# Moving ScalarE's splitting copies of the rotary queries and keys one to five heads later

## The chip, the cores and the metric

One core of a Trainium2 chip runs the whole kernel as one program. The metric is the device time of one execution in microseconds: the kernel before took 1350.16 us (median of 3 runs, 1348.41 to 1352.78). The engines are TensorE (PE), VectorE (DVE), ScalarE (ACT), GpSimd (POOL) and SyncE (SP), which issues most transfers. Each has its own instruction queue, runs it strictly in order, and waits on semaphores that the other engines and the transfers raise.

## The reference

Two layers of a gated decoder on x (8 sequences of 256 rows, 256 features). Layer 0 is a decoder block (masked self-attention, cross-attention, feed-forward) and a mixture of experts, top 2 of 8. Layer 1, cut to what matters here:

```
x = x + tanh(g_xattn[1]) * rotary_cross_attention(layernorm(x), ctx, key_mask)
x = x + tanh(g_ffn[1])   * moe_top1_of_8(layernorm(x))

q = larope(x @ Wq + bq);  k, v = split(ctx @ Wkv + bkv);  k = larope(k)
attn = softmax(q k^T / 8, masked keys off);  out = (attn v) @ Wo + bo      # 16 heads of 16 features
```

`larope` turns each pair of features by an angle that grows with the position: te*cos - to*sin, te*sin + to*cos.

## The kernel before

The stage of the change is the function `rotary_and_experts`: the rotary cross-attention of layer 1, sequence by sequence, and then the top-1 experts on sorted rows. The order of all engines in it is written out by hand as loops over a **beat** b (0 to 7, the sequence whose softmax is made) and within it a **head** h (0 to 15). In head h of beat b TensorE makes the transposed scores of (b, h) (`scores_T`, L1228) and the plain scores of a head eight further on (`scores`, L1210: sequence b+1, head h+8, or from h = 8 on sequence b+2, head h-8). VectorE takes their row maxima (L1774), and ScalarE makes the exponential of the transposed scores (`exps`, L1491). TensorE may start `scores_T` of head h once the exponential of head h-2 is done (two banks). Between the heads stand the other steps of several sequences:

- sequence b+3, queries: TensorE's product at h = 0 (L1177), VectorE's rotation at h = 0 (L1758, L1760), then the **split** in three bf16 parts, so that scores in bf16 keep float32 precision: GpSimd adds the two halves (`whole`, L1603), ScalarE copies to bf16 (`first_part`, L1467), GpSimd makes the remainder (`rest`, L1608), ScalarE copies it (`second_part`, L1472), GpSimd makes the third part (`third_part`, L1613).
- sequence b+3, keys: product and rotation at h = 4, the same split.
- sequence b+3, values: product at h = 8 (`project_values`, L1200), ScalarE's copy (`value_rows`, L1484), GpSimd's column of ones (`keep_values`, L1631).
- sequence b-1: heads are transposed at h = 6, ScalarE copies them (`bring_heads`, tile `aT`, L1460), output product at h = 12. Several products share two banks in a fixed rotation; the value product of h = 8 needs the bank that `bring_heads` empties.
- sequence b+4: rows are transposed at h = 10; ScalarE copies them (`bring_rows`, L1454).
- sequence b-2: new row norm, whose inverse roots GpSimd makes in fourteen small operations (`inverse_roots`, L134 to L141, from beat 2 on), and VectorE applies at h = 9. Routing of sequence b-3 follows, with GpSimd's scatter (L1639).
- at h = 1, 5, 9, 13 ScalarE copies out four heads' attention output (`outputs`, L1497), which TensorE transposes two heads later (L1259).

GpSimd's order in a beat is: roots of sequence b+4, the whole split of the queries (sum, remainder, third part), roots of sequence b-2, the whole split of the keys, `keep_values`, from beat 4 on weight loads of the experts (`load_expert`, L1049 and L1050, 2 MB per expert; expert 0 in beat 4, experts 1 to 3 in beat 5), then the scatter.

SP's order in beat b is: query stacks, key stacks and key row of sequence b+2 (`stack`, L1066 and L1069, loads from DRAM in the layout that the scores want; they wait for the end of beat b-1 and for the parts' writes to have landed), the write of the query parts of b+3 to DRAM (`spread_parts`, L1077, waits for the third part), the two small transfers of the maxima (L1081, L1082), the write of the key parts of b+3, in beat 0 two further small ones (L1132, L1133), and from beat 2 on the rows of sequence b-2 kept for the router (L1087, two transfers). The first use of the stacks of sequence b+2 is `scores` at h = 8 of beat b.

ScalarE in head h does its exponential, then the split steps, then `bring_heads`, `bring_rows`, router copies and `outputs`.

Of the kernel before, what the change touches and what calls it, by code (L numbers as in the profile page):

```python
# [970 lines left out]
def rotary_and_experts(nc, tag, c, mem, X, Y, L, gate, x_dram, gate_f, ids_dram, rows_dram, out, w1_in, w2_in, b1_in, b2_in, wg_in, bg_in):  # L971
# [10 lines left out]
    with ExitStack() as ctx:  # L982
# [466 lines left out]
        def _(act):  # L1449
            def bring_rows(m):  # L1450
                if m >= 1:
                    act.wait_ge(*full("q", m - 1))
                act.wait_ge(*full("x", m))
                nc.scalar.activation(flat(xT[:, :, :]), bank_of("x", m)[:, :], ACT.Copy).then_inc(emptied("x", m), 1)  # L1454

            def bring_heads(m):
                if m >= 1:
                    act.wait_ge(*full("z", m - 1))
                act.wait_ge(*full("a", m))
                nc.scalar.activation(flat(aT[:, :, :]), bank_of("a", m)[:, :], ACT.Copy).then_inc(emptied("a", m), 1)  # L1460

            def first_part(m, side):
                f, parts, at = ((fq, pq, q_place), (fk, pk, k_place))[side]
                act.wait_ge(f_sum[side], m + 1)
                if m >= 1:
                    act.wait_ge(spread[side], 16 * m)
                nc.scalar.activation(flat(parts[:, at[0], :, :]), f[:, :], ACT.Copy).then_inc(part1[side], 1)  # L1467

            def second_part(m, side):
                r, parts, at = ((rq, pq, q_place), (rk, pk, k_place))[side]  # L1470
                act.wait_ge(rest1[side], m + 1)
                nc.scalar.activation(flat(parts[:, at[1], :, :]), r[:, :], ACT.Copy).then_inc(part2[side], 1)  # L1472

            def value_rows(m):
                p = m % 4
                act.wait_ge(*full("v", m))
                if m >= 4:
                    act.wait_ge(pv_done, QUADS * (m - 3) + 2)
                if m == 0:
                    act.wait_ge(ready0, 1)  # L1480
                    act.wait_ge(kept_in, 1)
                for u in range(NU):
                    rows = V[:, p, u, 0:H * VW].rearrange("p (h e) -> p h e", e=VW)
                    ins = nc.scalar.activation(rows[:, :, 0:DK], bank_of("v", m)[:, u * D:(u + 1) * D].rearrange("p (h e) -> p h e", e=DK),  # L1484
                                               ACT.Copy, scale=mcf[:, m * NU + u:m * NU + u + 1])
                ins.then_inc(emptied("v", m), 1)

            def exps(m, h):
                act.wait_ge(st_ready, H * m + h + 1)
                act.wait_ge(pv_done, QUADS * m + h // 4 + 1)  # L1490
                nc.scalar.activation(PT[h % 8], bankT[h % 2][:, :], ACT.Exp).then_inc(exp_done, 1)  # L1491

            def outputs(g):
                act.wait_ge(pv_done, g + 3)
                if g >= 2:
                    act.wait_ge(*full("o", g - 2))
                nc.scalar.activation(OTS[:, g % 2, :], bankO[g % 2][:, 0:SEQ], ACT.Copy).then_inc(ot_out, 1)  # L1497

            def bring_router(n):
                act.wait_ge(*full("t", n))  # L1500
                if n >= 1:
                    act.wait_ge(*full("l", n - 1))
                nc.scalar.activation(flat(yT[:, :, :]), bank_of("t", n)[:, :], ACT.Copy).then_inc(emptied("t", n), 1)

            def probabilities(n):
                act.wait_ge(centred, n + 1)
                nc.scalar.activation(expd[:, :, :], expd[:, :, :], ACT.Exp).then_inc(prob_done, 1)
# [43 lines left out]
            for b in range(0, M):  # L1551
                for h in range(H):
                    exps(b, h)
                    if has(b + 3):
                        if h == 2:
                            first_part(b + 3, 0)
                        if h == 4:
                            second_part(b + 3, 0)
                        if h == 6:
                            first_part(b + 3, 1)  # L1560
                        if h == 8:
                            second_part(b + 3, 1)
                            value_rows(b + 3)
                    if h == 6 and has(b - 1):
                        bring_heads(b - 1)
                    if h == 10 and has(b + 4):
                        bring_rows(b + 4)
                    quad = QUADS * b + (h - 5) // 4
                    if h == 6 and early(b - 3):
                        probabilities(b - 3)  # L1570
                    if h == 15 and early(b - 2):
                        bring_router(b - 2)
                    if b == M - 1 and h == 12:
                        bring_router(EARLY_ONES - 1)
                    if h in PV_AT and 0 <= quad < QUADS * M:
                        outputs(quad)
# [1208 lines left out]
```

## Time and profile before

| what | value |
|---|---|
| median of 3 runs | 1350.16 us (1348.41 to 1352.78) |
| profiled execution | 1353.81 us, its span 1352.0 us |
| TensorE busy | 1181.2 us, 87% |
| VectorE busy | 786.6 us, 58% |
| ScalarE busy | 624.9 us, 46% |
| GpSimd busy | 554.8 us, 41% |
| mean granted TensorE clock | 0.945 |

Times in the rows are microseconds from the start of the span. Beat 0 begins at 948.9 (ScalarE's first exponential), beat 2 at 993.5, beat 5 at 1076.6, and the last beat ends near 1142. The span is the time from the first to the last instruction; the execution is 1.8 us longer. An entry in brackets is the engine's idle time just before the instruction and what ended it. `L_W` is the big memory that holds stacks, parts and, later, expert weights, so many tiles print by this one name; the line number tells them apart.

### The profile page before, as it was taken

The page shows a single profiled execution, that of the slowest core. Times are in us where ns is not written, and L with a number is a line of the kernel's source. Part 1 is how long each engine was busy: PE and PEld are TensorE (multiplying, and loading weights), DVE is VectorE, ACT ScalarE, POOL GpSimd, SP SyncE. Part 2 cuts the span into 40 slices and gives each one's busy share as a digit, 9 for nine tenths or more (in the row PEclk, how much of TensorE's full clock was granted, in tenths as well). Part 3 has the DMA queues.
Part 4 walks back from the last instruction along what each step waited for, and adds up shares of the span by engine and source line. Part 5 has one row for each costly group of instructions (what it writes and reads, how often), then busy time and mean ns, then how long its engine had stood idle before and what let it go on. Part 6 is the DMA issues. An engine that isn't in the chain of part 4 may idle for free. (4 is left out here: it accounts for less than half of the span.)

```text
span 1352.0 us, 27251 instructions
## 1 busy us (share of the span) xinstructions
PE 1181.2 (87%) x8333; PEld 944.7 (70%) x8333; DVE 786.6 (58%) x2994; ACT 624.9 (46%) x1515; POOL 554.8 (41%) x927
## 2 busy tenths in 40 slices
PE   4599999999997999899999999346988868689996
PEld 3366667676654888789999999333656645689995
DVE  4588878888873488855333333226868866532231
ACT  2268777888885332233333333011555535233331
POOL 3334454545433344545333333145454433433431
PEclk9799999999997999999999999776899989899998
DMA  4766674545411971132222222287434785511110
GB/s 107 176 128 169 144 171 101 116 98 117 97 36 22 378 197 33 48 45 36 37 41 35 37 40 31 40 180 176 100 84 114 152 248 188 188 34 48 39 36 6
DMA packets 116790, 137.64 MB, mean 102 GB/s; under 512 B 25739, under 2 KB 103065, under 8 KB 111740
## 3 DMA queue, kind: packets, MB, share of 16 engines
q1 hardware_dynamic: 101416, 106.73, 33.3%
q0 software_dynamic: 15232, 29.17, 9.6%
q8 instruction: 70, 1.15, 0.4%
q14 instruction: 72, 0.59, 0.2%
HBM read 102.51 MB, written 35.97 MB: 102 GB/s over the span
## 5 line engine op out<-in xcount | busy, mean ns | idle before, releaser
L765 DVE CUSTOM_DVE_ANT_0 att_masked_scores<-att_S,Bm 128x256 bf16<-128x256 f32 x512 | 190.2, 419 | 38.2 <-PE att_S L507 26.7
L640 ACT ACTIVATE att_PT<-att_T 128x512 f32<-128x512 f32 x256 | 146.3, 591 | 50.1 <-PE att_T L529 46.2
L2401 ACT ACTIVATE moe_hT<-moe_H,moe_b 128x128 f32<-128x128 f32 x312 | 89.2, 369 | 170.2 <-PE moe_H L2314 168.9
L2326 PE MATMUL moe_Z<-moe_W,moe_hT 128*128 x624 | 141.6, 380 | 0.8 <-DVE moe_z L2626 0.8
L2489 POOL DMA_INDIRECT x<-Y,X x39 | 62.5, 1602 | 156.3 <-DVE Y L2637 152.0
L2326 PEld LDWEIGHTS moe_Z<-moe_W,moe_hT 128*128 128x128 f32 x624 | 115.5, 190 | 15.5 <-issue 1.2
L507 PE MATMUL att_S<-L_KS,L_QS 96*128 96x256 bf16 x512 | 99.2, 276 | 21.3 <-DMA L_KS<-att_k_dram 14.7
L1774 DVE TENSOR_REDUCE out_mx<-out_S 128x2 f32<-128x512 f32 x128 | 85.2, 685 | 28.6 <-PE out_S L1210 27.9
L529 PE MATMUL att_T<-L_QS,L_KS 99*128 99x256 bf16 x512 | 97.9, 273 | 4.0 <-ACT att_T L645 3.7
L2314 PEld LDWEIGHTS moe_H<-moe_aT,ff_w 128*128 128x128 f32 x832 | 96.8, 192 | 4.0 <-issue 2.1
L2314 PE MATMUL moe_H<-moe_aT,ff_w 128*128 128x128 f32 x832 | 97.2, 275 | 2.3 <-DVE X L2621 1.7
L2626 DVE TENSOR_TENSOR moe_z<-moe_Z,moe_b 128x256 f32<-128x256 f32 x39 | 16.6, 424 | 141.8 <-PE moe_Z L2326 141.8
L1525 ACT ACTIVATE X<-out_T,L_b 128x128 f32<-128x128 f32 x184 | 52.5, 369 | 97.6 <-PE out_T L1339 97.1
L1491 ACT ACTIVATE L_W<-out_T 128x512 f32<-128x512 f32 x128 | 72.6, 596 | 38.6 <-PE out_T L1228 38.0
L1339 PEld LDWEIGHTS out_T<-out_xT,L_w1s 128*128 128x128 f32 x736 | 86.6, 194 | 4.4 <-issue 1.9
L1339 PE MATMUL out_T<-out_xT,L_w1s 128*128 128x128 f32 x736 | 87.4, 278 | 2.7 <-DVE L_w1s L1915 1.4
L1352 PE MATMUL out_S<-L_W,X 128*128 x368 | 83.5, 380 | 2.4 <-DVE out_ys L1924 2.4
L645 ACT ACTIVATE att_T<-BmT 128x512 f32<-128x512 bf16 x127 | 76.4, 602 | 4.0
L1352 PEld LDWEIGHTS out_S<-L_W,X 128*128 128x128 f32 x368 | 68.1, 190 | 11.8 <-issue 3.5
L1210 PE MATMUL out_S<-L_W 97*128 97x256 bf16 x256 | 53.6, 297 | 24.4 <-DVE out_mx L1774 13.9
L507 PEld LDWEIGHTS att_S<-L_KS,L_QS 96*128 96x128 bf16 x512 | 45.9, 98 | 39.3 <-DMA L_KS<-att_k_dram 15.9
L529 PEld LDWEIGHTS att_T<-L_QS,L_KS 99*128 99x128 bf16 x512 | 49.4, 99 | 32.1 <-ACT att_T L645 6.8
(451 smaller groups left out, 2550.3 us busy)
## 6 DMA issues: line engine op xcount, KB each, us to landing
moe_W<-in_L_ffn_W SPq DMA_DIRECT2D x16, 1024.0 KB, 13.0
L_W<-in_L_ffn_W POOLq DMA_DIRECT2D x12, 1024.0 KB, 11.5
att_q_dram<-att_pq SPq DMA_DIRECT2D x16, 384.0 KB, 4.0
att_k_dram<-att_pk SPq DMA_DIRECT2D x16, 384.0 KB, 2.8
L_QS<-att_q_dram SPq DMA_DIRECT2D x16, 384.0 KB, 4.7
L_KS<-att_k_dram SPq DMA_DIRECT2D x16, 384.0 KB, 8.1
L_QS<-att_q_dram SPq DMA_DIRECT2D x16, 256.0 KB, 5.6
L_KS<-att_k_dram SPq DMA_DIRECT2D x16, 256.0 KB, 8.6
```

What stands on the lines that cost most here:

```text
L507: ins = nc.tensor.matmul(bankS[h % 2][:, u * SEQ:(u + 1) * SEQ], QS[0:ROWS, m % 3, h, u * P:(u + 1) * P], KS[0:ROWS, m % 3, h, :], start=T ...
L529: ins = nc.tensor.matmul(dst[:, u * SEQ:(u + 1) * SEQ], KS[0:ROWS_ALL, m % 3, h, u * P:(u + 1) * P], QS[0:ROWS_ALL, m % 3, h, :], start=Fa ...
L640: nc.scalar.activation(PT[:, h % 8, :], bankT[h % 2][:, :], ACT.Exp).then_inc(exp_done, 1)
L645: nc.scalar.activation(bankT[1][:, :], masks[layer][1][:, :], ACT.Copy).then_inc(seeded, 1)
L765: ins = nc.vector.tensor_tensor_reduce(masked_scores[:, h % 2, u, :], bankS[h % 2][:, u * SEQ:(u + 1) * SEQ], masks[m // B][0][:, u * SEQ: ...
L1339: ins = nc.tensor.matmul(bankH[half][:, f * P:(f + 1) * P], matrix[:, cc, k * P:(k + 1) * P], xT[:, s % 2, cc * P:(cc + 1) * P], start=(cc ...
L1352: ins = nc.tensor.matmul(bankY[:, 0:D], eT[:, s % 2, f * P:(f + 1) * P], matrix[:, f, :], start=(f == 0), stop=(f == NF - 1))
L1491: nc.scalar.activation(PT[h % 8], bankT[h % 2][:, :], ACT.Exp).then_inc(exp_done, 1)
L1774: nc.vector.tensor_reduce(mx[:, m % 2, :, h:h + 1], bankS[h % 2][:, :].rearrange("p (u k) -> p u k", u=NU), AXX, ALU.max).then_inc(max_don ...
L2314: ins = nc.tensor.matmul(bankH[half][:, f * P:(f + 1) * P], matrix[:, cc, g * P:(g + 1) * P], xT[:, s % 2, cc * P:(cc + 1) * P], start=(cc ...
L2326: ins = nc.tensor.matmul(bankZ[:, 0:D], eT[:, s % 2, f * P:(f + 1) * P], w2e[:, f, :], start=(f == 0), stop=(f == NF - 1))
L2401: ins = nc.scalar.activation(eT[:, s % 2, g * P:(g + 1) * P], bankH[half][:, f * P:(f + 1) * P], ACT.Relu, bias=b1[:, bass.ds(e * NF + g, 1)])
```

## The change

In beats 0 to 4 (those with a sequence b+3) ScalarE's four copies of the split move: queries' first part from head 2 to 3, queries' second from 4 to 6, keys' first from 6 to 9, keys' second from 8 to 13. `value_rows` stays at head 8. Nothing else is touched: the orders of TensorE, VectorE, GpSimd and SP are as before.

```diff
                 for h in range(H):
                     exps(b, h)
                     if has(b + 3):
-                        if h == 2:
+                        if h == 3:
                             first_part(b + 3, 0)
-                        if h == 4:
+                        if h == 6:
                             second_part(b + 3, 0)
-                        if h == 6:
+                        if h == 8:
+                            value_rows(b + 3)
+                        if h == 9:
                             first_part(b + 3, 1)
-                        if h == 8:
+                        if h == 13:
                             second_part(b + 3, 1)
-                            value_rows(b + 3)
                     if h == 6 and has(b - 1):
                         bring_heads(b - 1)
```

## Rows read from the trace of the kernel before

**Rows 1.** Windows: us, busy us (instructions) per engine, granted clock, DMA share, GB/s
```profile
993.50:1023.30 29.80, 24.49 (x184) 16.97 (x182) 20.33 (x54) 14.53 (x30) 12.85 (x36) 0.89 0.45 100
1076.60:1107.20 30.60, 19.04 (x169) 12.64 (x167) 18.30 (x56) 11.47 (x25) 9.71 (x22) 0.83 1.03 276
1009.40:1015.60 6.20, 6.20 (x30) 4.15 (x30) 1.52 (x4) 2.72 (x6) 2.08 (x4) 0.52 0.00 0
```

**Rows 2.** Timeline of ScalarE in beat 2, from head 6 on
```profile
1003.44 0.60 ACT L1491 ACTIVATE L_W<-out_T 128x512 f32<-128x512 f32 x1
1008.18 0.63 ACT L1467 ACTIVATE L_W<-L_W 128x512 bf16<-128x512 f32 x1 [4.15 <-POOL L_W L1603]
1008.72 0.58 ACT L1460 ACTIVATE out_aT<-out_A 128x512 f32<-128x512 f32 x1
```

**Rows 3.** Timeline of GpSimd in beat 2: third part, first root operation, sum
```profile
1001.85 1.17 POOL L1613 TENSOR_TENSOR L_W<-L_W 128x512 bf16<-128x512 f32 x1 [0.74 <-ACT L_W L1472]
...
1003.11 0.21 POOL L134 TENSOR_SCALAR out_ve<-out_mv 128x2 f32<-128x2 f32 x1
...
1006.89 1.26 POOL L1603 TENSOR_TENSOR L_W<-L_W 128x512 f32<-128x512 f32 x1
```

**Rows 4.** Timeline of TensorE in beat 2: value projection, head 12
```profile
1009.35 3.78 PE L1200 MATMUL out_A<-L_W 128*128 128x256 f32 x8 [4.13 <-ACT out_aT L1460]
...
1017.26 0.38 PE L1228 MATMUL out_T<-L_W 99*128 99x256 bf16 x2
```

**Rows 5.** Timeline of SP's transfer issues, beats 0, 1, 4 and 5
```profile
967.42 0.54 SPq L1132 DMA_DIRECT2D ids<-out_none  x1
...
970.17 1.25 SPq L1066 DMA_DIRECT2D L_W<-out_q_dram  x3
...
972.85 0.49 SPq L1069 DMA_DIRECT2D L_W<-key_off  x1
...
1052.42 0.52 SPq L1069 DMA_DIRECT2D L_W<-key_off  x1
...
1070.45 0.53 SPq L1077 DMA_DIRECT2D out_k_dram<-L_W  x1
...
1075.62 1.37 SPq L1066 DMA_DIRECT2D L_W<-out_q_dram  x3
```

**Rows 6.** Transfers, last column us to landing: key row in 969:974, in 1049:1054
```profile
L_W<-key_off SPq DMA_DIRECT2D x1, 8.0 KB, 9.1
...
L_W<-key_off SPq DMA_DIRECT2D x1, 8.0 KB, 12.0
```

**Rows 7.** Timeline of TensorE at head 8 of beats 1, 4 and 5
```profile
982.00 0.38 PE L1210 MATMUL out_S<-L_W 97*128 97x256 bf16 x2
983.12 1.99 PE L1200 MATMUL out_B<-L_W 128*128 128x256 f32 x8 [0.73 <-ACT out_aT L1460]
...
1064.92 0.38 PE L1210 MATMUL out_S<-L_W 97*128 97x256 bf16 x2
...
1096.00 0.58 PE L1210 MATMUL out_S<-L_W 97*128 97x256 bf16 x2 [9.85 <-issue]
```

**Rows 8.** All 16 parts' writes to DRAM (L1077)
```profile
DMA to landing us min/median/max: 2.7/3.0/13.9
```

**Rows 9.** Timeline of GpSimd: first half of load 0
```profile
1068.82 0.82 POOL L1049 DMA_DIRECT2D L_W<-in_L_ffn_W  x1
```

**Rows 10.** Timeline of ScalarE in beat 3: exponential of head 6
```profile
1036.28 0.60 ACT L1491 ACTIVATE L_W<-out_T 128x512 f32<-128x512 f32 x1
```

**Rows 11.** Timeline of TensorE in beat 3: head 12
```profile
1044.18 0.38 PE L1228 MATMUL out_T<-L_W 99*128 99x256 bf16 x2
```

**Rows 12.** Timeline of ScalarE: heads 11 to 13 of beat 0, head 13 of beat 4
```profile
967.12 1.67 ACT L1491 ACTIVATE L_W<-out_T 128x512 f32<-128x512 f32 x3
...
1073.20 0.60 ACT L1491 ACTIVATE L_W<-out_T 128x512 f32<-128x512 f32 x1 [1.80 <-PE out_T L1228]
```

**Rows 13.** SP's queue in 1084:1097: packets, MB, share of 16 engines
```profile
q1 hardware_dynamic: 282, 1.22, 40.8%
```

## The prediction

> **What bounds the kernel now.** I read the busy time by windows first, one window per rotary beat. Beats 2 and 5 stand out: 29.80 and 30.60 us long, TensorE busy 24.49 and 19.04 of them, at a mean granted clock of 0.89 and 0.83 [rows 1]. The question is what TensorE waits for there.
>
> Beat 2 is read from the timelines of three engines. ScalarE's exponential of head 6 starts at 1003.44. Next on its queue is the first part of the keys, which starts only at 1008.18, idle 4.15 us before it, released by GpSimd; behind that sits the copy `aT` (`bring_heads`), at 1008.72 [rows 2]. GpSimd explains the wait: the third part of the queries at 1001.85, then the fourteen small operations of the inverse root from 1003.11, then the sum of the keys at 1006.89, 1.26 us [rows 3]. TensorE's value projection needs the bank that `aT` empties: it starts at 1009.35, idle 4.13 before it [rows 4]. From 1009.4 to 1015.6 the granted clock was 0.52, the lower level of 1.2 GHz, behind those four idle microseconds [rows 1]; the projection took 3.78 us at that level [rows 4], and half of it, 1.9, would do at 2.4 GHz (the 1.99 of beat 1's row, [rows 7]). So the stall costs its own length and some 2 us more.
>
> Then the transfers. At the top of beat b SP reloads the stacks of sequence b+2: queries, keys, and last the key row (L1069). In beat 1 that row is issued at 972.85 and lands 9.1 us later, at 981.95 [rows 5, 6]; TensorE's first scores from it (head 8) start at 982.00 [rows 7]. In beat 4 it lands 12.0 us after its issue at 1052.42, so at 1064.4, and the scores start at 1064.92 [rows 5 to 7]. These loads arrive just in time: there is a hidden second bound. In beat 5 it shows: scores start at 1096.00, idle 9.85 [rows 7]. The key stack may go only when the key parts' write to DRAM (issued 1070.45, [rows 5]) has landed, and this one took 13.9 us, where the median is 3.0 [rows 8]: until 1084.35. Load 0 of the experts (2 MB by its shapes), which GpSimd issued at 1068.82 [rows 9], came ahead of it.
>
> **The change part by part.** No instruction is added or removed; ScalarE's order moves in beats 0 to 4.
>
> First part of queries, head 2 to 3: one exponential of 0.6 us goes before it, and its wait for GpSimd's sum shrinks by as much. TensorE runs ahead of ScalarE by two heads here and did not wait. I take 0; bounds 0 and -0.6 a beat, one exponential.
>
> First part of keys out of head 6. The second part of queries takes its slot, but needs only a remainder finished long before, so `aT` starts 0.63 us after the head-6 exponential and no longer after GpSimd. Beat 2: exponential ends 1004.04, second part to 1004.67, `aT` to 1005.25, projection at 1005.3 rather than 1009.35. But the GpSimd chain now starts later: third part of queries 1004.7 to 1005.9 (1.17, [rows 3]), roots 3.8 us (1003.11 to 1006.89) to 1009.8, sum 1.26 to 1011.1, first part of keys at head 9 to 1011.7, output copy 0.3, exponential of head 10 to 1012.6. TensorE's own work from the projection to head 12 took 7.9 us, 1009.35 to 1017.26 [rows 4], 6.2 of them at half clock; at full clock it is 4.8, so TensorE would be ready at 1010.1 and waits for that exponential: head 12 starts at 1012.65 instead of 1017.26 [rows 4], -4.6 us. Upper bound of the gain: head 12 right behind its own work, 1010.1, -7.2; lower: if the clock still falls, -3. I take -4.6, for every term of it is a row.
>
> Beats 3 and 4: the same chain, but the old stall was small there: from the exponential of head 6 to TensorE's head 12 it is 1036.28 to 1044.18, 7.9 us, in beat 3 [rows 10, 11], where beat 2 took 13.8. New in beat 3: second part of queries to 1037.5, third to 1038.75, roots to 1042.6, sum to 1043.9, first part of keys to 1044.6, copy 0.3, exponential of head 10 to 1045.5; head 12 starts 1045.6 instead of 1044.18. +1.4; bounds 0 (TensorE's lead of two heads hides it) and +2.8 (beat 4 pays it too; in my sum it is covered there by the late stacks). In beats 0 and 1 GpSimd has no such roots and the chain is 3.8 us shorter: 0. `bring_heads` is also earlier in beat 1, which the next term swallows.
>
> Second part of keys, head 8 to 13. This is the step with the price. Behind it on GpSimd stand the third part of the keys (1.2 us), the value columns, the scatters and load 0; behind that third part on SP stands the write of the key parts (L1077), and behind that write, in order, the rows kept for the router, both query stacks and the key stacks of the next beat. Before, SP issued that write long before the stacks (1070.45 and 1075.62 in beats 4 and 5, [rows 5]). Now:
>
> Beat 0 to 1: heads 11 to 13 end at 968.8 [rows 12]; second part to 969.4, third to 970.6, write issued 970.7 (0.53), two more transfers of 0.54 to 0.7 [rows 5], query stacks at 972.6 instead of 970.17 [rows 5], +2.4. Key row lands at 984.4 instead of 981.95, and TensorE had no slack: scores at 984.5 instead of 982.00. The projection behind them starts at 984.75 and not 983.12 [rows 7], so the net is +1.6; bounds 0 (the transfers overlap better) and +2.5.
> Beat 1 to 2: the same working, less the two extra transfers, gives query stacks 1.1 us later. Beat 2's head 8 may be that much later at no cost, since TensorE waits for ScalarE from 1010.1 to 1012.6 there. 0; bounds 0 and +1.
> Beats 2 to 5: head 13's exponential starts 2.4 us before the query stacks (1073.20 and 1075.62, [rows 5, 12]; the order of heads 13 to 15 is the same in beats 2 and 3); 0.6 + 0.6 + 1.2 us for the three steps and 0.5 + 1.2 for the write and the kept rows, with 0.1 at each handover, make 4.4: the stacks leave 2.0 later.
> Beat 3 has room for it: its head 6 comes 13 us after the top of the beat (1023.3 and 1036.28, [rows 10]), head 8 some 2.4 later, and from the first stack's issue to the last landing beat 1 took 11.8. 0; bounds 0 and +1.
> Beat 4 has none: landing 1066.4 instead of 1064.4, wanted at 1064.92, so +1.5; the scatter, which stands behind the third part on GpSimd, now falls into this load, for which I add 0.3. +1.8; bounds 0 and +4.
> Beat 5: from head 13 at 1073.20 second part to 1074.4, third to 1075.6, write issued 1075.65 and load 0 at 1076.05, 7.2 us later than its 1068.82. The write now starts ahead of the load, a plus. But load 0 no longer moves in the 7 us before the stacks; write, kept rows, query and key stacks, 0.4 + 0.5 + 0.8 + 0.8 = 2.5 MB by their shapes on SP's queue, now stand in front of beat 5's need together with load 0 and then loads 1 to 3. From 1084 to 1097 SP's queue moved 1.22 MB in 13 us beside the loads [rows 13], 94 KB/us. Some 0.3 MB (my estimate: one microsecond or two at the beginning) go before load 0 begins; 2.15 MB at 94 to 110 KB/us take 19.5 to 23 us from 1077.7: 1097 to 1101. If the small pieces are held back behind load 0 as before and the stacks begin at 1086, 1.54 MB end at 1100 to 1102. I take 1101, +5.0. Bounds: -5 (the early write lands in 3 us, key stacks leave at 1079 and land in 12, as in beat 4) and +11 (the rates fall to 70 KB/us, since beside load 0 the small pieces got less than the stacks do).
>
> Load order is where a rule bears. The row shows a write of 384 KB at 13.9 us beside load 0 against 3.0 at the median [rows 8]. The Trainium skill, "DMA: Bandwidth & Descriptors", section "Queues, rings and completion order", says that each engine alternates between queues a packet at a time, and that a semaphore's increment lands only after every earlier write of that engine, from whatever queue. By the second half, a write issued just ahead of load 0 would land unhindered, which makes the -5 end a rival; by the first, the stacks share with the loads from then on, which is the +5 term. The row of 13.9 us agrees with the rule; no row shows a write issued just ahead of a load.
>
> Sum: -4.6 + 1.4 + 1.6 + 1.8 + 5.0 = +5.2 us. Against the profiled execution's 1353.8: 1359.0. That execution lies 3.6 over the median of the runs, 1350.2; on the median: 1355.4.
>
> **The rivals.** No change: the write ahead of load 0 gives back what the later stacks lose, beat 5 starts its scores at 1096 as before, and the rest is +0.2: 1350.4. For it: every late term is of the size of beat 2's gain. Against: SP's queue holds 2.5 MB where it had 1.5.
> Faster: the write lands in 3 us as it does at its median [rows 8], key stacks leave at 1079 and land at 1091, and beat 4's load is not delayed beyond its slack: -4.6 + 1.4 + 1.6 + 0 - 5 = -6.6: 1343.6. It decides if load 0 yields to stacks that are already queued. For it: 13.9 us is four times the usual. Against: beat 4's loads took 12 us with no expert load beside them.
> Much slower: the stacks get only the smaller share until loads 1 to 3 are through, scores in beat 5 at 1107: +11 instead of +5: 1361.4. For it: the 1.22 MB in 13 us. Against: the stacks are then the larger of the two demands.
>
> **How the numbers follow.** Forecast 0.42, no change 0.21, faster 0.26, much slower 0.11. About 4 us, 0.3%, is what a measurement can tell from no change. The forecast lies just beyond it, so 0.05 of its 0.42 fall to "same"; of the 0.21 of no change, 0.02 fall to faster and 0.01 to slower. Faster 0.28, same 0.23, slower 0.49. The range, 1344 to 1361, runs from the faster rival to the much slower one; the forecast's own is 1351 to 1360.
>
> **What would show it.** Right: in beat 2 the idle time before the projection (L1200) is gone and the clock stays at 1.0; a wait of 2 to 3 us before the first keys part at head 9 in beats 2 to 4, on GpSimd's sum; SP's key write issued 1 to 2 us after ScalarE's second part; scores of head 8 idle 2 us in beat 1, on the key stacks. Wrong: beat 5's idle time under 8 us means that the order of write and load decides; beat 1 without that wait means that the stacks' landing does not follow their issue.

## The result, and the profile after

The changed kernel takes 1355.55 us (median of 22 runs), the kernel before, run beside it, 1350.15 (22 runs): ratio 1.0037, interval 1.0025 to 1.0049, so 5 us slower. The profiled executions are 1355.05 and 1353.81 us, only 1.2 apart, because the one of before was slower than any of its 22 runs (1344.19 to 1353.76). A second trace of each kernel was therefore taken, and the stage is read from all four.

First, by windows, beats 1 to 5 of the kernel after (us, busy us with instructions of TensorE, weight loads, VectorE, ScalarE, GpSimd, then granted clock, DMA share, GB/s):

```profile
970.50:993.30 22.80, 20.91 (x181) 15.00 (x179) 20.06 (x49) 13.85 (x28) 10.10 (x22) 1.00 0.50 114
993.30:1020.20 26.90, 23.76 (x184) 16.17 (x182) 21.63 (x55) 14.24 (x30) 12.86 (x36) 0.94 0.43 91
1020.20:1047.00 26.80, 23.62 (x195) 16.50 (x195) 24.52 (x69) 14.44 (x32) 13.58 (x37) 1.00 0.48 110
1047.00:1073.80 26.80, 22.80 (x193) 16.13 (x193) 22.34 (x64) 13.92 (x31) 12.32 (x26) 1.00 0.60 109
1073.80:1108.20 34.40, 19.13 (x169) 12.79 (x167) 18.41 (x56) 11.40 (x25) 12.65 (x25) 0.75 1.03 296
```

Against [rows 1], beat 2 went from 29.80 to 26.90 us and beat 5 from 30.60 to 34.40. In beat 5 TensorE does the same work and the rest is waiting.

**Beat 2** is read from three timelines, in the order of [rows 2 to 4]. ScalarE: `aT` (L1460) follows the exponential of head 6 at once, and the wait on GpSimd's sum stands before the first keys part at head 9 instead, 2.01 us:

```profile
1003.28 0.60 ACT L1491 ACTIVATE L_W<-out_T 128x512 f32<-128x512 f32 x1
1003.77 0.62 ACT L1472 ACTIVATE L_W<-L_W 128x512 bf16<-128x512 f32 x1
1004.29 0.59 ACT L1460 ACTIVATE out_aT<-out_A 128x512 f32<-128x512 f32 x1
...
1010.80 0.63 ACT L1467 ACTIVATE L_W<-L_W 128x512 bf16<-128x512 f32 x1 [2.01 <-POOL L_W L1604]
1011.34 0.37 ACT L1497 ACTIVATE out_OTS<-out_O 128x256 f32<-128x256 f32 x1
```

GpSimd: the third part now waits 3.52 us for ScalarE, and the root operations and the sum behind it are 2.6 us later than in [rows 3] (1004.47 for 1001.85, 1009.51 for 1006.89):

```profile
1004.47 1.15 POOL L1614 TENSOR_TENSOR L_W<-L_W 128x512 bf16<-128x512 f32 x1 [3.52 <-ACT L_W L1472]
...
1009.51 1.26 POOL L1604 TENSOR_TENSOR L_W<-L_W 128x512 f32<-128x512 f32 x1
```

TensorE: the projection (L1200) starts at 1005.54 with no wait for `aT`, 1.89 us long; head 12 starts at 1012.25. The wait has changed place: 1.39 us before L1259, whose input is the output copy queued behind the keys part:

```profile
1005.54 1.89 PE L1200 MATMUL out_A<-L_W 128*128 128x256 f32 x8
...
1011.76 0.44 PE L1259 MATMUL out_B<-ident,out_OTS 128*128 128x128 f32 x2 [1.39 <-ACT out_OTS L1497]
1012.25 0.39 PE L1228 MATMUL out_T<-L_W 99*128 99x256 bf16 x2
```

**Beat 5** starts at 1073.8 here and at 1076.6 in the trace before, so the issues are compared by their distance from it. SP issues the key write 1.1 us ahead of the beat (1072.73) instead of 6.2 (1070.45), and the query stacks 0.8 us into it (1074.63) instead of 1.0 ahead (1075.62) [rows 5], 1.8 later:

```profile
1072.73 0.38 SPq L1077 DMA_DIRECT2D out_k_dram<-L_W  x1
...
1074.63 2.03 SPq L1066 DMA_DIRECT2D L_W<-out_q_dram  x3
1076.76 2.18 SPq L1066 DMA_DIRECT2D L_W<-out_k_dram  x3
```

GpSimd issues the first half of load 0 at 1072.92, right after the write and not 1.6 us before it as in [rows 9]; against its beat that is 6.9 us later:

```profile
1071.56 1.15 POOL L1614 TENSOR_TENSOR L_W<-L_W 128x512 bf16<-128x512 f32 x1 [3.38 <-ACT L_W L1472]
...
1072.92 0.82 POOL L1049 DMA_DIRECT2D L_W<-in_L_ffn_W  x1
```

The transfers issued in 1072:1097 (last column: median us to landing) and, above them, what the two queues moved (packets, MB, share): the write lands in 2.8 us, where it took 13.9 [rows 8], but the stacks and the key row need 12.0 to 17.8 (before, 7.6 to 11.5):

```profile
q0 software_dynamic: 954, 3.46, 49.0%
q1 hardware_dynamic: 1648, 2.50, 46.0%
...
out_k_dram<-L_W SPq DMA_DIRECT2D x1, 384.0 KB, 2.8
L_W<-out_q_dram SPq DMA_DIRECT2D x1, 384.0 KB, 12.0
L_W<-out_k_dram SPq DMA_DIRECT2D x1, 384.0 KB, 15.9
...
L_W<-key_off SPq DMA_DIRECT2D x1, 8.0 KB, 17.8
```

TensorE at head 8 of beats 1, 4 and 5, to set beside [rows 7]: the wait of 9.85 in beat 5 is now 13.55, and beats 1 and 4 have short waits that were not there:

```profile
982.84 0.38 PE L1210 MATMUL out_S<-L_W 97*128 97x256 bf16 x2 [1.12 <-DMA L_W<-key_off]
983.06 1.89 PE L1200 MATMUL out_B<-L_W 128*128 128x256 f32 x8
...
1062.95 0.38 PE L1210 MATMUL out_S<-L_W 97*128 97x256 bf16 x2 [2.04 <-issue]
...
1096.87 0.59 PE L1210 MATMUL out_S<-L_W 97*128 97x256 bf16 x2 [13.55 <-issue]
```

### The profile page after: what moved, and what is told of

Its sections match the earlier page's. It is cut to its first block and busy times, and to the rows that moved or that the text cites. A ratio compares the mean times of both kernels' runs of the same rounds, so it can differ in the third digit from the quotient of the medians.

```text
span 1353.3 us, 27205 instructions
## 1 busy us (share of the span) xinstructions
PE 1174.0 (87%) x8287; PEld 942.8 (70%) x8333; DVE 789.0 (58%) x2994; ACT 623.8 (46%) x1515; POOL 554.4 (41%) x927
## 3 DMA queue, kind: packets, MB, share of 16 engines
q8 instruction: 70, 1.15, 0.4%
## 5 line engine op out<-in xcount | busy, mean ns | idle before, releaser
L529 PE MATMUL att_T<-L_QS,L_KS 99*128 99x256 bf16 x512 | 97.9, 273 | 11.5 <-ACT att_T L645 3.9
L1210 PE MATMUL out_S<-L_W 97*128 97x256 bf16 x256 | 54.0, 299 | 30.5 <-issue 15.6
```

The source lines that it names most:

```text
L529: ins = nc.tensor.matmul(dst[:, u * SEQ:(u + 1) * SEQ], KS[0:ROWS_ALL, m % 3, h, u * P:(u + 1) * P], QS[0:ROWS_ALL, m % 3, h, :], start=Fa ...
```

## All kernels by beat

Each beat is measured in the trace from ScalarE's first exponential to the next beat's first. "Stage" runs from beat 0's start to the last exponential; from there to the end of the span it is 210.2 to 211.4 us in every kernel. Heads are those of q1, q2, k1, k2 (first and second part of queries, then of keys). The ratio is to the kernel before, run in the same session.

| kernel | heads | beats 0 to 6 | stage | median us (runs) | ratio, interval |
|---|---|---|---|---|---|
| before | 2,4,6,8 | 21.9 22.7 29.8 27.2 26.2 30.5 18.2 | 192.6 | 1350.15 (22) | |
| same_before | 2,4,6,8 | 21.2 22.7 28.6 27.2 26.3 27.0 19.5 | 188.6 | 1352.89 (1) | |
| after | 3,6,9,13 | 21.8 22.9 26.8 26.8 26.8 34.4 18.2 | 193.9 | 1355.55 (22) | 1.0037, 1.0025–1.0049 |
| same_after | 3,6,9,13 | 22.1 25.2 25.2 26.8 29.9 33.3 19.3 | 198.0 | 1355.21 (11) | 1.0046, 1.0026–1.0065 |
| k2_at_10 | 3,6,9,10 | 22.6 22.7 28.0 27.9 26.3 31.1 18.2 | 192.8 | 1353.71 (12) | 1.0033, 1.0016–1.0050 |
| only_k2_at_13 | 2,4,6,13 | 21.9 25.0 28.5 26.9 27.3 34.3 18.2 | 198.3 | 1357.01 (7) | 1.0069, 1.0043–1.0094 |
| k_at_9_and_10 | 2,4,9,10 | 22.6 22.8 23.5 27.6 25.8 32.0 18.2 | 188.6 | 1345.74 (12) | 0.9975, 0.9959–0.9991 |
| k_at_9_and_13 | 2,4,9,13 | 21.5 23.0 22.9 26.6 26.6 34.0 18.2 | 189.0 | 1349.63 (12) | 1.0013, 0.9999–1.0028 |
| only_queries | 3,6,6,8 | 23.5 26.1 32.0 34.1 33.6 25.1 18.2 | 208.7 | 1368.59 (5) | 1.0146, 1.0125–1.0167 |
| load0_early | 3,6,9,13 | 22.1 25.7 25.2 26.8 27.5 27.7 18.2 | 189.2 | 1348.13 (12) | 1.0009, 0.9993–1.0024 |
| loads_wait | 3,6,9,13 | 21.4 23.1 26.6 26.9 29.2 27.5 19.0 | 189.4 | 1345.21 (12) | 0.9985, 0.9963–1.0006 |
| before_loads_wait | 2,4,6,8 | 21.9 22.7 29.4 27.2 26.1 22.7 19.1 | 184.8 | 1344.61 (12) | 0.9967, 0.9948–0.9986 |
| k_9_10_loads_wait | 2,4,9,10 | 22.6 22.6 23.5 27.6 25.8 22.6 19.4 | 180.8 | 1340.07 (9) | 0.9946, 0.9928–0.9965 |
| k_9_11_loads_wait | 2,4,9,11 | 20.7 22.2 22.5 27.3 26.6 23.2 19.5 | 177.9 | 1337.84 (6) | 0.9923, 0.9904–0.9941 |

The kernel before took 1349.1 us (29 runs) beside same_after, k2_at_10, only_k2_at_13 and k_at_9_and_10, 1347.5 (32) beside load0_early, loads_wait, before_loads_wait and k_9_10_loads_wait, and 1348.92 (17) beside the other four. Even the start of beat 0, ahead of which nothing differs, lies anywhere from 944.1 to 951.6: so one span says little, and beat lengths say more.

## The experiments

**The two kernels again.** No edit, same_after and same_before.

> The changed kernel again, unaltered, for a second trace and time. Theory (the late second part of the keys costs more in beat 5 than the freed head 6 gives back in beat 2): 1.002 to 1.005 times the kernel before; beat 2 shorter by about 3 us than the 29.8 before, idle time before beat 5's first scores (L1210) 13 to 15 us against 9.85. Rival (the +5 of the median is spread over the whole kernel and the beats are even, as the one profiled pair with its +1.3 suggests): beat 5 changes from trace to trace by as much as it differs from before.

> The kernel before again, unaltered, for a second trace of it. Theory (the profiled execution of before, 1353.8, was a slow one): the same waits at the same places, idle 4.1 us before beat 2's value projection and 9 to 10 us before beat 5's first scores, and a beat or two without a half-clock stretch that the first trace has or the other way round. Rival (beat 5's idle time is itself what varies): it is 7 us or less here.

Beat 5 waits 11.82 us in the second trace of after and 6.80 in that of before, in place of 13.55 and 9.85. So 13 to 15 us were not reached, and for before the rival came true: the wait of beat 5 itself varies by 3 us with the same code. TensorE, same_after:

```profile
1060.88 0.59 PE L1210 MATMUL out_S<-L_W 97*128 97x256 bf16 x2 [2.49 <-issue]
...
1096.84 0.37 PE L1210 MATMUL out_S<-L_W 97*128 97x256 bf16 x1 [11.82 <-issue]
```

and same_before:

```profile
1093.91 0.37 PE L1210 MATMUL out_S<-L_W 97*128 97x256 bf16 x1 [6.80 <-issue]
```

The shorter wait of same_before is not a faster write. The trace has no landing for it, but SP waited 6.0 us for it and could issue the key stacks only 12.6 us behind it (issued 1071.31):

```profile
1083.89 2.12 SPq L1066 DMA_DIRECT2D L_W<-out_k_dram  x3
```

What differs is the order behind it. Here the key stacks left 0.7 us ahead of GpSimd's load 1 (1084.58) and took 5.7 to 7.6 us; in the first trace they left at 1084.41, 0.7 behind it (1083.75), and took 7.6 to 10.1. That this order makes the 3 us is likely and not tested alone.

In beats 1, 2 and 4 what differs within one kernel is the clock. Windows of same_after:

```profile
967.20:992.50 25.30, 22.72 (x182) 16.02 (x182) 20.33 (x49) 14.13 (x30) 10.22 (x23) 0.93 0.47 102
992.50:1017.70 25.20, 21.99 (x184) 15.09 (x182) 21.58 (x54) 14.22 (x30) 12.90 (x36) 1.00 0.47 98
1044.40:1074.40 30.00, 25.47 (x193) 17.80 (x193) 22.43 (x64) 14.13 (x31) 12.75 (x26) 0.89 0.55 98
```

Here beats 1 and 4 ran partly at the lower level of 1.2 GHz, behind waits of 1.81 and 2.49 us, and beat 2 wholly at 2.4, behind a wait of 1.33 before L1259; in the trace of after it was the other way round (0.94 in beat 2, 1.00 in 1 and 4, behind 1.39, and 1.12 and 2.04). Such a beat is 1.6 to 3.1 us longer than in the other trace (26.8 for 25.2, 25.2 for 22.9, 29.9 for 26.8); in beats 1 and 4 the longer wait itself, 0.7 and 0.45 us, is in the difference. In beat 2 nearly all of it is one product: the eight matmuls of L1280 took 3.42 us in after and 1.97 in same_after. The mean stage of the two traces is 190.6 before and 196.0 after: +5.4, the same as the medians' +5.4. The traced pair alone gives +1.3.

**The second keys part alone, and its late place taken back.**

```diff
# k2_at_10: from after
-if h == 13:
+if h == 10:
     second_part(b + 3, 1)

# only_k2_at_13: from before (value_rows stays at h == 8)
-if h == 8:
+if h == 13:
     second_part(b + 3, 1)
```

> As the changed kernel, but the second part of the keys at head 10 instead of 13. Theory: the gain of beat 2 (-3) stays, and the write of the key parts, load 0 and the stacks go out about as before: beat 5's idle time back to about 10 us, so 3 to 4 us faster than the kernel before, 0.997. Rival 1 (ScalarE's and GpSimd's new chain at head 9 is what costs): no better than the changed kernel, 1.003. Rival 2 (any shift of load 0 costs): between them, 1.000.

> The kernel before with the second part of the keys alone moved, head 8 to 13. Theory: the loss without the gain: beat 5's idle time 13 to 15 us, beats 1 and 4 one to two us longer, beat 2 at its old 29.8; +6 to +9 us, 1.005 to 1.007. Rival (the late part is harmless, the loss sits in the new chain at head 9): 1.000.

Alone, the late part costs 1.0069, 9.3 us by the ratio and 7.9 between the medians, and shows all of the late terms: waits of 1.60 and 1.25 us in beats 1 and 4 and 11.83 us in beat 5, beside the old stall in beat 2 (3.33). TensorE, only_k2_at_13:

```profile
1012.59 0.80 PE L1200 MATMUL out_A<-L_W 128*128 128x256 f32 x1 [3.33 <-ACT out_aT L1460]
...
1068.64 0.38 PE L1210 MATMUL out_S<-L_W 97*128 97x256 bf16 x2 [1.25 <-issue]
...
1101.86 0.37 PE L1210 MATMUL out_S<-L_W 97*128 97x256 bf16 x1 [11.83 <-issue]
```

But k2_at_10 failed its expectation (0.997; measured 1.0033): taking the lateness back gains only 1.5 us on after. ScalarE of k2_at_10 shows the wait of head 9, and TensorE the two waits behind it, the second for the rows' copy:

```profile
1013.61 0.63 ACT L1467 ACTIVATE L_W<-L_W 128x512 bf16<-128x512 f32 x1 [2.52 <-POOL L_W L1604]
...
1014.57 0.44 PE L1259 MATMUL out_B<-ident,out_OTS 128*128 128x128 f32 x2 [1.89 <-ACT out_OTS L1497]
...
1016.77 0.45 PE L1280 MATMUL out_A<-L_wo,out_aT 128*128 128x256 f32 x1 [1.10 <-ACT out_xT L1454]
```

So something else of the change costs time in beat 2: 28.0 us.

**The queries left where they were.**

```diff
# k_at_9_and_10: from before; k_at_9_and_13 the same with 13 for 10
-if h == 6:
+if h == 9:
     first_part(b + 3, 1)
-if h == 8:
+if h == 10:
     second_part(b + 3, 1)
     # value_rows(b + 3) stays at h == 8
```

> The kernel before with the keys' parts alone moved: first part head 6 to 9, second 8 to 10; the queries stay at heads 2 and 4. Theory: GpSimd's chain (third part of the queries, roots, sum) starts as early as before, so ScalarE finds the sum ready at head 9 and has no new wait; beat 2 loses its whole stall and the half-clock stretch: -6 in beat 2, -1 in beats 3 and 4, 0.994 to 0.996. Rival (the gain of head 6 has to be paid with the same wait elsewhere): like k2_at_10, 0.997.

> The kernel before with the keys' parts alone moved, to heads 9 and 13; the queries stay at 2 and 4. It is the changed kernel without its moves of the queries. Theory (late second part: +6; freed head 6: about -3.5; the queries' moves cost by lengthening GpSimd's chain): 1.001 to 1.003, some 2 to 4 us faster than the changed kernel, no wait before the first keys part at head 9. Rival (the second part at 13 costs only the 1 us that separates the changed kernel from k2_at_10): 0.998.

With keys at 9 and 10 and the queries untouched beat 2 takes 23.5 us at a clock of 1.00, and the kernel is faster, 0.9975, though less than the 0.994 to 0.996 expected. The first keys part finds its sum ready:

```profile
1008.55 0.60 ACT L1491 ACTIVATE L_W<-out_T 128x512 f32<-128x512 f32 x1
1009.04 0.63 ACT L1467 ACTIVATE L_W<-L_W 128x512 bf16<-128x512 f32 x1
```

The second part at 13 in place of 10 costs 0.9975 to 1.0013, 5 us, with the queries early; its beat 5 is 34.0 for 32.0, beat 4 26.6 for 25.8. TensorE, k_at_9_and_13:

```profile
980.25 0.38 PE L1210 MATMUL out_S<-L_W 97*128 97x256 bf16 x2 [1.27 <-DMA L_W<-key_off]
...
1089.70 0.59 PE L1210 MATMUL out_S<-L_W 97*128 97x256 bf16 x2 [10.92 <-issue]
```

**The queries alone.**

```diff
# only_queries: from before
-if h == 2:
+if h == 3:
     first_part(b + 3, 0)
-if h == 4:
+if h == 6:
     second_part(b + 3, 0)
```

> The kernel before with the queries' parts alone moved, to heads 3 and 6; the keys stay at 6 and 8. Theory (GpSimd makes third part, roots and sum one after the other, and ScalarE waits for the sum at head 6): the wait before the first keys part grows by about 2.5 us in beats 2 to 4, to 7 us in beat 2, and stands ahead of the copy aT; +7 to +12 us, 1.005 to 1.009. Rival (the moves of the queries are harmless, as the step from k_at_9_and_10 to k2_at_10 came from the keys' second part at head 10): 1.000 to 1.002.

1.0146, 20 us slower, where at most 1.009 was expected. The sum of the keys is now needed at head 6 while the queries' second part is itself at head 6: third part, roots and sum all lie between the two on GpSimd, and ScalarE waits 6.39 us, TensorE 6.90 (before: 4.15 and 4.13, [rows 2, 4]). ScalarE:

```profile
1014.04 0.63 ACT L1467 ACTIVATE L_W<-L_W 128x512 bf16<-128x512 f32 x1 [6.39 <-POOL L_W L1602]
```

TensorE:

```profile
1015.21 0.79 PE L1200 MATMUL out_A<-L_W 128*128 128x256 f32 x1 [6.90 <-ACT out_aT L1460]
```

The same happens in beats 3 and 4 (5.85 and 5.63), which are 34 us long. Beat 5 is short, 25.1, with a wait of 3.62 us; that the longer beat 4 gives its stacks the time is argued, not tested.

**Load 0 before the third part.** This asks whether beat 5's loss is the late write or the load that now meets the stacks.

```diff
# load0_early: from after, GpSimd's loop
-parts(b + 3, 1)
+whole(b + 3, 1)
+rest(b + 3, 1)
+if b == 4:
+    first_expert()
+third_part(b + 3, 1)
 ...
-if b == 4:
-    first_expert()
```

> The changed kernel, but GpSimd issues load 0 of the experts in beat 4 before the keys' third part (behind their remainder) and not after it, so about where the kernel before issued it; the key parts' write stays late. Theory (load 0 takes the transfer engines in the very stretch in which the stacks of sequence 7 are wanted): load 0 is mostly through when the stacks leave, idle time before beat 5's first scores 7 to 10 us instead of 12 to 13.6, and the kernel at 1.001 to 1.003 of before. Rival (the lateness of the write itself is what costs in beat 5): idle time still 12 to 14 us, 1.004 to 1.005.

Load 0 starts at 1065.67 and the write is as late as in after, relative to its beat; beat 5 drops from 33.3 or 34.4 to 27.7, the wait to 6.97, and the kernel from 1.0037 and 1.0046, the two measurements of after, to 1.0009. The write, now 4.6 us behind the load, took 6.2 us:

```profile
1087.83 0.59 PE L1210 MATMUL out_S<-L_W 97*128 97x256 bf16 x2 [6.97 <-issue]
```

So most of what beat 5 paid was for the late load, not for the late write.

**No expert load until the last stacks have landed**, on after and on before.

```diff
# loads_wait, before_loads_wait: GpSimd's loop
-if b == 4:
-    first_expert()
 if b == 5:
+    for side in range(2):
+        pool.wait_ge(stacked[side][(M - 1) % 3], 16 * N_STACK[side] * ((M - 1) // 3 + 1))
+    first_expert()
     second_expert()
```

> The changed kernel, but load 0 moves to beat 5, and loads 0 to 3 wait there until the stacks of sequence 7 have landed. Theory (the stacks alone need about 9 to 12 us from their issue): idle time before beat 5's first scores 3 to 5 us instead of 12 to 13.6, and 8 to 10 us off the whole kernel, 0.996 to 0.998 of before, if the later loads are still in time for the expert slots. Rival (the stacks are late by their own write, the loads only keep them company): idle time 10 us or more, 1.003 to 1.005.

> The kernel before with the same wait for loads 0 to 3 and ScalarE's old order. Theory: the idle time of 9.85 us before beat 5's first scores was made by load 0 holding up the write and by loads 1 to 3 holding up the key stacks; it shrinks to 0 to 3 us, no half-clock stretch behind it: 0.992 to 0.994. Rival (the later loads are missed in the slots): a new wait for w_ready of some microseconds behind the last beat, 0.997 or more.

The stacks now have the transfer engines to themselves. On before the wait of beat 5 falls to 2.60 us; on after to 6.24, over the 3 to 5 expected: the 3.6 us between the two are what the later write and stacks cost in beat 5 with no expert load beside them. A small new wait of beat 7 for the maxima (L1082) appears: they took 6.8 us to land beside the loads (7.0 in before_loads_wait, 5.5 in before), 1.8 at the median. TensorE, loads_wait:

```profile
1090.58 0.37 PE L1210 MATMUL out_S<-L_W 97*128 97x256 bf16 x1 [6.24 <-issue]
...
1120.85 0.39 PE L1228 MATMUL out_T<-L_W 99*128 99x256 bf16 x2 [1.17 <-DMA L_W<-out_MT]
```

and before_loads_wait:

```profile
1086.69 0.38 PE L1210 MATMUL out_S<-L_W 97*128 97x256 bf16 x2 [2.60 <-issue]
```

It gains 1.0037 or 1.0046 to 0.9985 on after, 7 to 8 us (0.996 to 0.998 was expected), and 0.9967 on before, 4.4 us, less than the 0.992 to 0.994 expected: 2.60 us of waiting remain and the maxima's wait (1.34 in before_loads_wait) is new. From the last exponential to the end it is no longer than in the other kernels, so the experts lose nothing by the later loads.

**Both gains together.** Keys at 9 and 10, or 9 and 11, queries untouched, and the loads' wait.

```diff
# k_9_11_loads_wait: from before; k_9_10_loads_wait with 10 for 11
-if h == 6:
+if h == 9:
     first_part(b + 3, 1)
 if h == 8:
-    second_part(b + 3, 1)
     value_rows(b + 3)
+if h == 11:
+    second_part(b + 3, 1)
 # and the wait of before_loads_wait
```

> The candidate that beats both: queries' parts at heads 2 and 4, keys' at 9 and 10, and loads 0 to 3 behind the stacks of sequence 7. Theory: the two gains add, since they lie in different beats (2 and 5): 0.989 to 0.992. Rival (they share a cause): no better than before_loads_wait.

> The best so far (k_9_10_loads_wait, 0.9946) with the second part of the keys one head later, 11. Theory: the copy of the rows at head 10 no longer stands behind the second part, the key parts' write leaves 0.5 to 1.5 us later, still before the stacks: 0.993 to 0.995. Rival (each head later costs in the stacks): 0.996 or more.

1340.07 and 1337.84 us, 0.9946 and 0.9923: both beat both kernels. The gains add as measured, 0.9975 by 0.9967 is 0.9942, but both are smaller than expected, and so is their sum (0.989 to 0.992 was expected); 11 came out a little better than its 0.993 to 0.995. Their intervals overlap, so 11 against 10 is not decided. TensorE, k_9_11_loads_wait, beat 5:

```profile
1079.52 0.38 PE L1210 MATMUL out_S<-L_W 97*128 97x256 bf16 x2 [2.15 <-issue]
```

## Why the prediction was right, step by step

The total was right: +5.2 forecast, +5.4 between the medians. Set against the mean of the two traces of each kernel:

| step | forecast | measured | the two traces of after |
|---|---|---|---|
| beat 1, stacks later | +1.6 | +1.4 | 22.9, 25.2 |
| beat 2, stall before `aT` | -4.6 | -3.2 | 26.8, 25.2 |
| beat 3, wait at head 9 | +1.4 | -0.4 | 26.8, 26.8 |
| beat 4, stacks later | +1.8 | +2.1 | 26.8, 29.9 |
| beat 5, stacks beside load 0 | +5.0 | +5.1 | 34.4, 33.3 |
| sum | +5.2 | +5.0 | |

Two samples a side make these means good to some 2 us a beat, no better (beat 5 of before alone was 30.5 and 27.0). The forecast was worked from the first trace of before alone. Against that trace the five beats come to +1.3 in one trace of after and +4.0 in the other; the +5.0 needs the second trace of before, whose beats 2 and 5 were 1.2 and 3.5 us shorter. And within the sum beat 2 was forecast 1.4 us too good and beat 3 1.8 us too bad, which cancel. So the mechanisms of beats 2 and 5 were right, and that the total agrees to 0.2 us is luck. Of the signs named, the wait before head 9 was 2.01 us in beat 2, 1.61 in beat 3 and nothing in beat 4, for 2 to 3 in all three, and the wait of beat 1 was 1.12 and 1.81, for 2.

**Beat 2.** The mechanism and its times held: `aT` at 1004.29 and the projection at 1005.54 (forecast 1005.3 after a head-6 exponential 0.16 us later), the sum at 1009.51 for 1009.8, TensorE ready at 1010.4 for 1010.1 (1011.76 less its wait of 1.39), head 12 at 1012.25 for 1012.65. "The clock stays at 1.0" failed in the first trace: it fell behind the 1.39 us that remain of the wait, and the beat got 3.0 shorter, the stated lower bound. In same_after it stayed, and the beat is 4.6 under [rows 1], the forecast value (3.4 under the 28.6 of same_before). What the lower level costs is seen in the output product behind head 12, L1280, 3.42 us for 1.97.

**The queries' move was taken too lightly.** The prediction counted its first part at 0 and the whole chain behind the second at 2.6 us in beat 2 (head 12 at 1012.65 where TensorE could have been ready at 1010.1) and 1.4 in beat 3, 4.0 together, and treated it as what the gain comes with. Measured, with keys at 9 and 10, it costs 8.0 us between the medians (1345.74 to 1353.71, good to some 3), of which beat 2 holds 4.5 (23.5 to 28.0) and the traced stages 4.2 in all; the rest is not located. With keys at 9 and 13 it is 3.2 or 4.5 us (1.0013 to 1.0037 or 1.0046), with keys at 6 and 8, 20. The upper bound, -7.2 for beat 2, was nearly reached once the queries stayed (23.5 and 22.9 against 29.8). Moving the keys' two copies alone, to 9 and 10, would have been a gain.

**Beat 3, and what the queries' first part gives back.** The added chain is there: 1.61 us before the keys part at 1039.29, and from head 6's exponential to TensorE's head 12 it is 9.0 us where it was 7.9 [rows 10, 11], +1.1 for +1.4. The beat is nevertheless no longer: head 6's exponential comes 11.6 us after its start (1020.2 to 1031.76), 13.0 before. The step that failed is the 0 for the queries' first part. Before, GpSimd's remainder of the queries (L1608) starts at the moment of VectorE's second normalization of rows (the row of L151 holds both), which then lasts until 0.15 us behind the remainder's end; the logits (L1845) come behind it, and TensorE's key product (L1177) waits for them:

```profile
1029.25 1.60 DVE L151 TENSOR_SCALAR Y<-X,out_xmv,out_xr 128x256 f32<-128x256 f32 x2
1029.55 1.15 POOL L1608 TENSOR_TENSOR L_W<-L_W 128x512 f32<-128x512 f32 x1 [0.74 <-ACT L_W L1467]
1031.21 1.97 PE L1177 MATMUL out_A<-L_W 128*128 128x256 f32 x8 [1.43 <-DVE L L1845]
```

With the queries' first part one head later the remainder starts 0.24 us later against the beat, behind the start of that normalization (after):

```profile
1026.13 0.73 DVE L151 TENSOR_SCALAR Y<-X,out_xmv,out_xr 128x256 f32<-128x256 f32 x2
1026.67 1.19 POOL L1609 TENSOR_TENSOR L_W<-L_W 128x512 f32<-128x512 f32 x1 [0.98 <-ACT L_W L1467]
1027.21 1.97 PE L1177 MATMUL out_A<-L_W 128*128 128x256 f32 x8 [0.55 <-DVE L L1846]
```

All fourteen traces agree: L151 takes 1.6 us in beat 3 and TensorE waits 1.4 in the eight with the queries' first part at head 2, and it takes 0.7 and TensorE waits 0.55 in the six with head 3. In seven of the eight the granted clock also fell within 1.2 us of the end of that wait; in none of the six did it fall there. So the move of the queries' first part gained some 1.4 us by head 6, 0.9 of them at this wait, and it is the second part, which GpSimd's third part waits for, that lengthens the chain. No run moved the first part alone. In beat 4 the keys part at 1066.31 waits for nothing.

**Beats 1 and 4.** Query stacks left at 972.07, forecast 972.6, and the key row landed after 7.2 us and not 9.1 [rows 6]; so the scores came 0.84 us later than in [rows 7], not 2.5. TensorE waited 1.12 or 1.81 us for the key row, and 2.04 or 2.49 in beat 4. Where the clock stayed up, the beats are only 0.2 and 0.6 us longer than before, below the +1.6 and +1.8 of the sum; the traces with the half-clock stretch, 2.3 and 3.1 us longer than those, lift the mean to them. That was no term of the sum; the size agrees partly by luck.

**Beat 5.** Right in mechanism. The stacks left 1.8 us later against their beat (forecast 2.0) and load 0 6.9 (forecast 7.2). The first scores came 23.1 and 22.5 us into the beat, where it was 19.4: +3.7 and +3.1 for +5.0. The mean of +5.1 is reached through the shorter beat 5 of same_before. The early write did land unhindered (2.8 us). That agrees with one half of the rule in the Trainium skill, "DMA: Bandwidth & Descriptors", section "Queues, rings and completion order", the one on earlier writes, which favoured the faster rival. The other half, that the queues take turns, agrees with what decided: SP's queue moved 2.50 MB in 25 us beside 3.46 MB of loads, 100 KB/us. The prediction took 94 to 110, of which [rows 13] show the 94; no row shows the 110. loads_wait shows the cost by removing the sharing alone: 7 to 8 us come back; load0_early, which takes load 0 alone out of the way, brings back 4 to 5. The later write and stacks cost 3.6 us even with no load beside them. The faster rival's first condition held (2.8 us), and it fails at its second, "if load 0 yields to stacks that are already queued"; it doesn't, since the same transfers took 12.0 to 17.8 us here and 8.3 to 10.7 in loads_wait. The much slower one fails since the stacks kept their share. What the prediction did not price is what the loads cost in the kernel before already: 4.4 us.

## What to carry to other kernels

When a copy blocks an in-order queue, move that copy past what it blocks, and leave what feeds it early unless a trace gives a reason: the queries' copies that were moved along with it made the chain on the other engine later (3 to 8 us here, net of 1.4 us that one of them gained), and the late end of the chain pushed a just-in-time transfer (5 us). Bulk loads with slack belong behind the landing of the small transfers that the next stage needs; issued 1.6 us ahead of the key write or 0.2 us behind it, they cost the stage some 4 and 7 to 8 us. Look also at what two engines do in the same half microsecond: a shift of 0.24 us was worth 0.9 us of the other engine's time. And a traced pair can differ by 1.3 us where medians differ by 5.4, so compare the same stage in two traces of each kernel before sizing terms.

## What the runs showed of the hardware that was not expected

- The granted clock fell behind waits of 1.39, 1.81 and 2.49 us in one execution or the other of after and stayed at 1.0 behind 1.12, 1.33 and 2.04 us, at the same places of the same code; it stayed even behind 2.67 us in beat 4 of load0_early. The beats with a stretch at 1.2 GHz were 1.6 to 3.1 us longer.
- A write of 384 KB landed in 13.9 us when issued 1.6 us behind a 1 MB load, in 6.2 us when issued 4.6 us behind the first of two such loads (load0_early), and in 2.8 us when issued 0.2 us ahead of one; 8 KB of maxima (L1082) took 5.3 to 7.3 us beside the loads (7.3 in k_9_10_loads_wait) and 1.8 without.
- A VectorE instruction of 0.41 us took 1.28 when a GpSimd instruction of 1.15 us had started 0.02 us ahead of it; it took 0.41 when the GpSimd one started 0.2 us behind it.
- The same key row landed 9.1 and 8.3 us after its issue in beat 1, in two traces of the kernel before.
